# Turning the quantised levels: TensorE and ScalarE against SyncE's transposing transfers, in a fused attention and feed-forward kernel

## The reference

```
a   = causal attention of layernorm(x), 16 heads of 32, with a decay of -(i - j) added to the scores
x1  = x + layernorm(a @ Wo.T + bo)
h   = layernorm(x1) @ H                  # H: 512 x 512 Hadamard matrix
s   = max(|h| over the row) / 7
q   = clip(round(h / s), -8, 7) * s      # 4-bit levels
out = x1 + layernorm(q @ ternary(weight).T)
```

## Time and profile before

| | |
|---|---|
| median of 3 runs | 1175.83 us (1175.19 to 1178.08) |
| the profiled execution: its own time | 1174.37 us |
| its span, first to last instruction | 1172.5 us |
| mean granted TensorE clock | 0.967 of full speed |
| PE busy | 1097.7 us (94%), 18656 matmuls |
| PEld busy | 734.6 us (63%) |
| DVE busy | 988.0 us (84%) |
| ACT busy | 707.5 us (60%) |
| POOL busy | 587.9 us (50%) |
| SP's and the other hardware queues: share of 16 DMA engines | 57.8% |
| chain that ended last | PE 72%, DVE 18%, issue 3%, DMA 2%, SPq 2% |

### The profile page before, as it was taken

One profiled execution on the slowest core, in us unless ns is written; L12 is line 12 of the kernel. 1 busy time (PEld: TensorE's weight loads), 2 busy tenths in 40 slices (PEclk: granted clock), 3 DMA queues, 4 the chain that ended last, 5 costly groups with the idle time before them and its releaser, 6 DMA issues.

```text
span 1172.5 us, 44910 instructions
## 1 busy us (share of the span) xinstructions
PE 1097.7 (94%) x18656; PEld 734.6 (63%) x18656; DVE 988.0 (84%) x2562; ACT 707.5 (60%) x1493; POOL 587.9 (50%) x715
## 2 busy tenths in 40 slices
PE   4899999999999999999999999999999999999552
PEld 3565666666666666666666666666667666665321
DVE  5748998889988888899888888898888889887574
ACT  5445666666666666665666666566666665675432
POOL 1333565565545655555546556555555565454421
PEclk9989999999999999999999999999999999999765
DMA  9648677756668676666576766557677666554221
GB/s 276 152 79 145 138 155 164 149 139 140 127 127 147 160 164 150 134 137 130 127 150 160 164 151 134 133 116 144 156 155 162 146 138 143 113 122 116 68 64 46
DMA packets 204831, 161.81 MB, mean 138 GB/s; under 512 B 150448, under 2 KB 150704, under 8 KB 204528
## 3 DMA queue, kind: packets, MB, share of 16 engines
q1 hardware_dynamic: 199888, 141.86, 57.8%
q0 software_dynamic: 4736, 17.04, 4.1%
HBM read 40.87 MB, written 16.78 MB: 49 GB/s over the span
## 4 chain that ended last, share of the span: by engine, by line
PE 72%; DVE 18%; issue 3%; DMA 2%; SPq 2%; ACT 1%; POOLq 1%; POOL 0%; DVEq 0%; ACTq 0%
PE f_job L1349 46%; PE f_st L1450 5%; PE f_o L1467 5%; PE f_o L1472 4%; PE f_job L1526 3%; PE f_job L1425 2%; PE f_job L1508 2%; DVE f_stage L948 2%; DVE f_bst L994 2%; DVE f_rmax L962 2%; PE f_job L1516 1%; DVE f_inverse L986 1%; DVE f_x L1038 1%; DVE f_o L984 1%; PE f_job L1433 1%
## 5 line engine op out<-in xcount | busy, mean ns | idle before, releaser
L481 POOL TENSOR_SCALAR_AFFINE_SELECT f_PT<-f_PT 64x512 f32<-64x512 f32 (+1 forms) x256 | 203.3, 812 | 160.6 <-ACT f_PT L647 109.4
L496 POOL TENSOR_TENSOR f_square<-f_stage 128x512 bf16<-128x512 f16 x128 | 131.1, 1047 | 90.9 <-ACT f_stage L625 78.5
L487 POOL TENSOR_TENSOR f_OTl<-f_o,f_OTh 128x256 f16<-128x256 f32 x127 | 84.6, 673 | 139.1 <-ACT f_OTh L665 139.1
L1349 PE MATMUL f_job<-f_xTh,f_wqh 128*128 128x256 f16 x512 | 140.8, 275 | 14.4 <-DVE f_wkl L823 14.3
L625 ACT ACTIVATE f_stage<-f_job,f_bias 128x256 f16<-128x256 f32 x256 | 106.6, 468 | 76.1 <-PE f_job L1349 69.3
L1349 PE MATMUL f_job<-f_xTl,f_wqh 128*128 128x256 f16 x512 | 140.1, 274 | 0.0
L1349 PE MATMUL f_job<-f_xTh,f_wql 128*128 128x256 f16 x512 | 140.1, 274 | 0.0
L1349 PE MATMUL f_job<-f_xTh,f_wkh 128*128 128x256 f16 x512 | 140.1, 274 | 0.0
L1349 PE MATMUL f_job<-f_xTh,f_wkl 128*128 128x256 f16 x512 | 140.0, 273 | 0.0
L1349 PE MATMUL f_job<-f_xTl,f_wkh 128*128 128x256 f16 x512 | 140.0, 273 | 0.0
L948 DVE SCALAR_TENSOR_TENSOR f_stage<-f_job,f_bias,f_stage 128x256 f16<-128x256 f32 x256 | 111.0, 476 | 32.9 <-ACT f_stage L625 32.8
(11 more groups left out here) (197 smaller groups left out, 2940.7 us busy)
## 6 DMA issues: line engine op xcount, KB each, us to landing
f_stacks<-f_stage SPq DMA_DIRECT2D x380, 128.0 KB, 4.0
f_xin<-x SPq DMA_DIRECT2D x32, 512.0 KB, 6.4
f_x<-x SPq DMA_DIRECT2D x32, 512.0 KB, 4.5
out<-f_z POOLq DMA_DIRECT2D x31, 512.0 KB, 3.5
f_Vmix<-f_V SPq DMA_DIRECT2D x32, 256.0 KB, 6.1
f_Vmix<-f_V SPq DMA_DIRECT2D x64, 128.0 KB, 6.2
f_stacks<-rows_const SPq DMA_DIRECT2D x3, 512.0 KB, 5.0
f_stacks<-wqT SPq DMA_DIRECT2D x2, 512.0 KB, 5.8
```

The costliest lines, as they stand in the source:

```text
L481: nc.gpsimd.affine_select(out=d, in_=d, compare_op=ALU.is_ge, fill=0.0, base=odd * SUB, pattern=[[0, 4], [0, TP], [1, SUB]], channel_multi ...
L487: nc.gpsimd.tensor_tensor(OT[s % 2][1][:, g, :], o32[:, g % 2, :], OT[s % 2][0][:, g, :], ALU.subtract).then_inc(OTl_made, 1)
L496: nc.gpsimd.tensor_tensor(square[:, 2 * m + pair, :], h, h, ALU.mult).then_inc(squared, 1)
L1349: mm = pe.matmul(dst, lhs[a](c), rhs[b](c), start=(n == 0), stop=(n == 3 * KC - 1))
```

## The change

In steps 0 to 28 (`by_queue = STEPS - 3`) the levels are no longer turned by TensorE and copied by ScalarE. SP issues one transposing transfer per tile, from `q16` straight to `qT` (`turn_levels`); the ternary product waits for that transfer (`q_moved[t]`) instead of for `keep_q`, and so does `x2_high`. In the loop `turn_q` and `keep_q` go away altogether (in the loop the levels are those of steps 0 to 28); steps 29 to 31, behind the loop, are turned as before.

SP's order within a pass changes too. Before: 12 pieces in the order of the parts 0, 1, 2. After: the four pieces of part 0; the turning of tile 0; pieces (1, 0), (2, 2), (1, 1), (2, 3); the turning of tile 1; pieces (1, 2), (2, 0), (1, 3), (2, 1), where (p, r) is piece r of part p. The first step's restack, ahead of the loop, keeps parts 0 and 1 as before (part 2 of it is issued by POOL in both kernels).

```diff
--- before.py
+++ after.py
@@ -240,6 +240,7 @@
         rounded = sem("rounded")
         q_made = sem("q_made")
         q_turned = sem("q_turned")
+        q_moved = [sem(f"q_moved{t}") for t in range(TP)]
         qT_made = sem("qT_made")
         f_product = sem("f_product")
         z_made = sem("z_made")
@@ -281,6 +282,12 @@
 
             return 0 <= s < STEPS
 
+        by_queue = STEPS - 3
+
+        def levels_read(k, t):
+
+            return (q_moved[t], 16 * (k + 1)) if k < by_queue else (q_turned, TP * (k - by_queue) + t + 1)
+
         def rows_of(t, s):
             return t[s // PER, s % PER * W2:(s % PER + 1) * W2, :].rearrange("(t p) n -> p t n", p=P)
 
@@ -345,6 +352,12 @@
                 for half, src in enumerate((x2h, x2l)):
                     sp.dma_start(x2T[half][:, t], src[:, t, :], transpose=True).then_inc(x2_turned[t], 16)
 
+            def turn_levels(k, t):
+
+                sp.wait_ge(q_made, TP * k + t + 1)
+                until(sp, f_product, TP * (k - 1) + t + 1)
+                sp.dma_start(qT[:, t], q16[:, t, :], transpose=True).then_inc(q_moved[t], 16)
+
             def load_res(k):
 
                 until(sp, out_made, TP * (k - 1))
@@ -354,12 +367,7 @@
                     sp.wait_ge(ff_step, FF_STEPS)
                 sp.dma_start(x1[k % 2][:], rows_of(x, k)).then_inc(xres_in[k % 2], 16)
 
-            def restack(n, part):
-
-                if part == 0:
-                    sp.wait_ge(qk_high, 8 * n + 8)
-                else:
-                    sp.wait_ge(qk_low, 8 * n + 8)
+            def stacks_free(n):
                 if n == 0:
                     sp.wait_ge(w_low, 4)
                 if n == 1:
@@ -369,8 +377,21 @@
                     sp.wait_ge(ff_step, FF_STEPS)
 
                 until(sp, keyed, 2 * 4 * (n - 1))
+
+            def restack_high(n):
+
+                sp.wait_ge(qk_high, 8 * n + 8)
+                stacks_free(n)
                 for r in range(4):
-                    sp.dma_start(*stack_piece(n, part, r)).then_inc(stacked, 16)
+                    sp.dma_start(*stack_piece(n, 0, r)).then_inc(stacked, 16)
+
+            def restack_low(n, steps, parts=2):
+
+                sp.wait_ge(qk_low, 8 * n + 8)
+                for r in steps:
+                    sp.dma_start(*stack_piece(n, 1, r)).then_inc(stacked, 16)
+                    if parts == 2:
+                        sp.dma_start(*stack_piece(n, 2, (r + 2) % 4)).then_inc(stacked, 16)
 
             def mix_values(n):
 
@@ -410,8 +431,8 @@
             sp.wait_ge(w_low, 4)
             load_rows(0)
             turn_x(1)
-            restack(0, 0)
-            restack(0, 1)
+            restack_high(0)
+            restack_low(0, range(4), 1)
             load_front(2)
             mix_values(0)
             sp.dma_start(had[:], had16).then_inc(consts_in, 16)
@@ -426,9 +447,13 @@
                     load_front(m + 1)
                 if s:
                     mix_values(s)
-                restack(n, 0)
-                restack(n, 1)
-                restack(n, 2)
+                restack_high(n)
+                if has(k - 1):
+                    turn_levels(k - 1, 0)
+                restack_low(n, (0, 1))
+                if has(k - 1):
+                    turn_levels(k - 1, 1)
+                restack_low(n, (2, 3))
                 if has(m):
                     turn_x(m)
                 if has(k):
@@ -667,7 +692,8 @@
 
             def x2_high(k, t):
                 act.wait_ge(folded, 2 * (TP * k + t) + 2)
-                until(act, q_turned, TP * (k - 1) + t + 1)
+                if k:
+                    act.wait_ge(*levels_read(k - 1, t))
                 nc.scalar.activation(x2h[:, t, :], folded_x[:, t, :], ACT.Copy, scale=SX).then_inc(x2h_made, 1)
 
             def round_levels(k, t):
@@ -680,7 +706,7 @@
                 nc.scalar.activation(q16[:, t, :], bank("h", t)[:], ACT.Identity, bias=unround_col[:]).then_inc(q_made, 1)
 
             def keep_q(k, t):
-                act.wait_ge(q_turned, TP * k + t + 1)
+                act.wait_ge(*levels_read(k, t))
                 until(act, f_product, TP * (k - 1) + t + 1)
                 nc.scalar.activation(qT[:, t], bank("q", t)[:, 0:D // 2].bitcast(BF16).rearrange("p (c n) -> p c n", c=KC),
                                      ACT.Copy).then_inc(qT_made, 1)
@@ -741,14 +767,11 @@
                 exps(s, 1, 1)
                 if has(k - 1):
                     round_levels(k - 1, 1)
-                    keep_q(k - 1, 0)
                 if s == 0:
                     keep_tern()
                 if has(k - 1):
                     level(k - 1, 1)
                 invert(s, 0)
-                if has(k - 1):
-                    keep_q(k - 1, 1)
                 invert(s, 1)
                 exps(s, 2, 0)
                 heads_high(s, 0)
@@ -1359,7 +1382,7 @@
                        "tern": lambda _, i: (tern_kept, 2 * i + 2),
                        "y": lambda k, t: (y_made, TP * k + t + 1),
                        "h": lambda k, t: (q_made, TP * k + t + 1),
-                       "q": lambda k, t: (qT_made, TP * k + t + 1), "f": lambda k, t: (z_made, TP * k + t + 1)}
+                       "q": lambda k, t: (qT_made, TP * (k - by_queue) + t + 1), "f": lambda k, t: (z_made, TP * k + t + 1)}
 
             def claim(kind, i, step):
 
@@ -1521,7 +1544,10 @@
                 claim("f", t, k)
                 if k == 0 and t == 0:
                     pe.wait_ge(tern_kept, KC)
-                pe.wait_ge(qT_made, TP * k + t + 1)
+                if k < by_queue:
+                    pe.wait_ge(q_moved[t], 16 * (k + 1))
+                else:
+                    pe.wait_ge(qT_made, TP * (k - by_queue) + t + 1)
                 for c in range(KC):
                     mm = pe.matmul(bank("f", t)[:], qT[:, t, c, :], ternT[:, c, :],
                                    start=(c == 0), stop=(c == KC - 1))
@@ -1564,8 +1590,6 @@
                     turn_tern()
                 if has(k):
                     out_product(k, 0)
-                if has(k - 1):
-                    turn_q(k - 1, 0)
                 keys(s, 1, 0)
                 keys(s, 1, 1)
                 if has(k):
@@ -1575,7 +1599,6 @@
                 weigh(s, 1)
                 keys(s, 2, 1)
                 if has(k - 1):
-                    turn_q(k - 1, 1)
                     second(k - 1, 0)
                 values(n, 0)
                 if has(k - 1):
```

## The result

The changed kernel takes 1192.69 us (median of 4 runs, 1188.93 to 1196.86), the kernel before 1176.53 in the same comparison: ratio 1.0137 [1.0121, 1.0153]. It is 1.4% slower where 0.9% faster was forecast, and lies above the range. The profiled execution is the longest of the four: 1196.86 us, span 1195.2 us, mean granted clock 0.966 (before 0.967).

A forecast was written before the change was run, and what follows sets the result against it. PE's issue was taken to bound each pass. From the profiled 1174.37 us, 13.05 off for the turnings and 2.7 added for restack waits gave 1164.0, or 1165.5 for the median of runs; range 1161 to 1177.

The forecast's parts named there:

- What leaves PE: Turning matmuls' starts on PE: 0.45 us per pass gained, 13.05 us over 29 passes, 10.2 at the low end.
- The 0.10 us: Product to keys against product to turning on PE: up to 0.10 us of the turnings' gain could be left there.
- What leaves ACT: Two 0.6 us copies per pass: worth 0 by itself; the levels of tile 1 come about 0.5 us sooner.
- larger of the two: End of restack issues (start S): SP's limit S + 10.4 or the DMA limit, S + 11.7 in the slowest pass, whichever is later.
- The last piece: Restack's last piece before `scores`: lands 3.1 us after issue, S + 12.9 in ordinary passes; 2.7 us of waiting in all.
- rival 2: Restack slips 4.0 us per pass, 2.7 to spare before `scores`: +38 us, 1214; slower, with rival 1's far end, 0.12.
- Rival 1: Last piece lands in 3.4 to 4.0 us, waits 7 to 18 us, about 1175; half its sizes 0.15, middle 0.13.
- `second` waits 0: PE's `second` for either tile's transfer: 0; landing up to 4.4 us after issue, late by up to 1.2 in the worst pass.
- the banks handed back earlier: Two PSUM banks of the turnings, for `values(n, 0)` and `scores(n, 0)`: condition met earlier, PE waited for neither, 0.
- `turn_x`: Transfer of x behind the restack: up to 2.5 us later, with 2 us to spare before the next `qk`.
- `x2_high`: Its wait for the transfers comes a whole scores pass later: 0.
- the alternation by itself: Alternating parts 1 and 2 changes which partitions neighbouring restack pieces write; no row shows the effect on rate: taken as 0.

The follow-up runs named there:

- no_turning: Changed kernel without its transposing transfers in steps 1 to 28, those levels left unturned: 1187.38 us, ratio 1.0097.
- after_late_mask: Complete changed kernel, with POOL waiting ahead of the mask of group 2 until DVE has folded: 1182.17 us, ratio 1.0057.
- parts_in_turn: Changed kernel with the low pieces in the old order of the parts, transfers still behind the fourth and eighth piece: 1201.72 us, ratio 1.0192.
- both_ways: Kernel before, PE and ACT untouched, plus the change's two transfers into a tile nobody reads; `x2_high` waits for them too: 1198.12 us, ratio 1.0179.
- order_alone: Kernel before with only the alternation of the pieces of parts 1 and 2: 1174.75 us, ratio 0.9982.
- left_out_late_mask: no_turning with POOL waiting ahead of the mask of group 2 until DVE has folded: 1167.85 us, ratio 0.9941.

## Why the prediction was wrong

**What leaves PE: right.** The junctions are 0.22 and 0.23 us shorter where PE doesn't wait (2.92 to 2.69, 0.58 to 0.35 in no_turning). The 0.10 us was counted as a possible loss and isn't one: 0.45 us per pass, 13.05 in all.

**What leaves ACT, "by itself worth 0": this step failed, and no rival covered it.** The prediction read ACT as an engine that PE never waits for, and priced its loss of work at nothing except the levels of tile 1. It did not ask what a freer ACT makes start earlier. The second `keep_q` waited for PE's second turning (28 times in the stretch, 23.4 us in all), ahead of the exponentials of group 2 and of POOL's mask behind them, and before the mask came behind DVE's small operation. Without `keep_q` the mask comes 0.9 us earlier and draws out DVE's chain, DVE reaches `scale_out` 0.88 us later in the pass (means 20.43 and 21.31), of which it had some 0.3 to spare, and `scores` waits 0.60. By itself, in no_turning, this is 1187.38 - 1167.85 = 19.5 us (18.3 by the ratios); in the changed kernel 0.8%, 9 to 10 us, since there PE waits at the same place for the restack anyway. The collision and its price are shown by the runs; that it is the wait of `keep_q` that kept the two apart is argued.

**What comes to SP: the "larger of the two" failed.** The prediction let the DMA engines catch up while SP stands in a transposing issue, so that ordinary passes end at S + 10.4. Not one does: the 28 end at S + 10.50 to 12.41, mean 11.55. The mean before was 8.66; the two transposing issues, 1.35 us each in the mean (1.25 in the median), bring it to 11.36, and the pieces take 0.19 longer. The issue time is added in full, even in passes of 9 us and more.

**The last piece, "at least 3.1, so I take 3.1": undersized.** It landed 4.04 us after its issue before (mean of 28), and 3.41 after: the queue does empty a little more, 0.63 us, and that is all that was caught up. Landed is S + 14.26, where the prediction had S + 12.9 for ordinary passes. What there was to spare before was 1.78 us on average, against a delay of 2.26: the sum of rival 2 with other numbers. Its place is right, its 4.0 us slip was too large and its 2.7 us to spare too. Rival 1 had the landing time right (3.4 is its lower end), but kept the issue term; both sizes failed together, and that case was priced by neither.

The prediction's own sum over the 29 passes tells the two apart (an estimate). With 2.5 us of issue added in full it gives 12.9 us of waiting instead of 2.7; with 3.41 us for the landing alone 7.2; with both 19.8, and so 1165.5 - 2.7 + 19.8 = 1182.6 us. That is where after_late_mask stands, 1182.17, which has the restack's wait without the collision. It is so close by some luck, since the sum leaves out the waits in front of `second`. The rest up to 1192.69, some 10 us, is the term of ACT.

**`second` waits 0: wrong, small.** The bound of 4.4 us for landing was the median of another transfer. The levels' own took

```profile
DMA to landing us min/median/max: 2.9/4.6/6.3
```

and PE waits 12 times, 5.0 us, partly for tile 0 (0.07 us per pass), mostly for tile 1 (0.20).

**Right at 0:** the banks handed back earlier, `turn_x`, `x2_high` and the alternation by itself (0.9982); under the transfers it may save some 6 us, as said at parts_in_turn.

**The sum by what the runs showed,** per pass of the profiled executions: -0.45 for the turnings; +0.27 in front of `second`; +0.65 in front of `scores`, +0.14 inside it; +0.10 in the value product of tile 1; +0.08 in small places: +0.79, which is 34.35 - 33.56. Over 28 to 29 passes that is 22.1 to 22.9 us, the 22.7 by which the spans differ (1195.2 - 1172.5). The median of the runs is 16.2 us longer, because the profiled execution was the longest.

**TensorE against DMA for the blocks.** The Trainium skill puts TensorE ahead of DMA for a 128 x 128 block ("VectorE: DVE Perf Modes", figures in the section "The three transpose paths", the rule in "Rules for kernel authors"). As a verdict this case bears it out: with the mask held back in both, the transfers cost 14.3 us, and the matmuls' starts were 13.05. Its figure, taken block by block, does not fit: eight blocks at 1309 ns would be 10.5 us per pass, an estimate from that page. Measured as packet time of SP's queue with the order of the pieces the same, 58 transfers add 98.2 us of 16 engines in both_ways (64.7% of 1199.2, 775.9, less 677.7), 1.7 us each, and 107.2 in the kernel after (63.2% of 1195.2, 755.4, less order_alone's 648.2), 1.85 each. Alone it was 0.66 to 0.81.

**What stays open.** Whether the 2.5 to 2.7 us of SP's issue or the 3.4 to 3.7 us of data per pass pushes the restack back. The ends of the issues speak for SP: the 12 pieces' own issues add up to 7.96 us before and 8.14 after, so they hardly slow down under the transfers. But no run separates the two. There is no measurement of copies with the issue and no data, of copies with the data and half the issue, of the late mask alone in the kernel before, of one tile turned by each way, or of one transfer for both tiles. No version that beats the kernel before and computes the same was found: order_alone is within 0.3%, and left_out_late_mask leaves work out.

## What to carry to other kernels

Ask of every wait and every copy that goes away what it was holding back: an engine with idle time can still set when another one's work starts, and two engines that never met will meet. If less work makes a kernel slower, look for an operation whose duration has changed though its form hasn't; a list of min/median/max per line shows it at once. On a queue that PE nearly waits for, add the full issue time of what is put in, and take the landing time of the last piece from the passes themselves, not its best case: the spare of 28 passes is read in the same view.

## What the runs showed of the hardware

- A DVE operation on 128x2 elements, 0.15 us otherwise, takes 0.61 us when it begins behind a running mask (AFFINE_SELECT) on POOL, and one of 128x256 takes 0.87 for 0.42. POOL's pair of masks takes 1.29 us where it meets nothing (mean of left_out_late_mask), 1.71 where it begins ahead of DVE's small operation, 2.71 where it begins behind it, in the folds. In each case the one that begins second is drawn out: in the kernel before DVE's operations keep their 0.15 and 0.42 us and the first mask takes 2.08 for 0.66; in no_turning the first mask still takes 0.84, having begun 0.32 us before DVE's residual ended. The Trainium skill ("SBUF — State Buffer", section "SBUF: two separate sides") says that the two share a port pair and that the one that starts first holds it for its whole instruction. The order of who pays here agrees.
- One mask can wait for a whole row of DVE operations. In the kernel before six folds follow one another, each beginning 0.08 us before the last one ends, and the first mask ends 0.53 us behind the last of them, whether it began 0.61 us behind the small operation or 1.38 (all 28 passes).
- A transposing transfer of 128 KB in the full queue: 1.25 us to issue (1.22 to 2.14), 4.6 us to landing (2.9 to 6.3), 1.7 to 1.9 us of all 16 engines. Alone it was 2.5 us and 0.7.
- The same 12 pieces with parts 1 and 2 alternating take 29.5 us less of the DMA engines over the kernel (648.2 for 677.7), and the kernel's time does not change.
